# Selected tokens in quadrants: scores and mix of the first gated feed-forward layer as 64-wide tiles of the array

## The reference

```python
B, T, _ = X.shape                       # 4, 512, 128; E = 8 experts, k = T // 8 = 64
logits = jax.nn.sigmoid(jnp.einsum('bth,eh->bte', X, Wr))
topk_vals, topk_I = jax.lax.top_k(logits.transpose(0, 2, 1), k)
Xg = jnp.take_along_axis(X, idx_flat[:, :, None], axis=1).reshape(B, E, k, H)
QKV = jnp.einsum('beki,eij->bekj', Xg, Wqkv)
# rope on the first 64 features of Q and K, by the position of the token
M = topk_I[..., :, None] >= topk_I[..., None, :]
scores = jnp.where(M, jnp.einsum('bekd,bemd->bekm', Q, K) / math.sqrt(HP), -jnp.inf)
AV = jnp.einsum('bekm,bemd->bekd', jax.nn.softmax(scores, axis=-1), V) * topk_vals[..., None]
Xpre = jnp.einsum('bekj,eji->beki', AV, Wo)
out = jnp.zeros((B, T, H)).at[jnp.arange(B)[:, None], idx_flat].add(Xpre.reshape(B, E * k, H))
```

## Time and profile before

| | us |
|---|---|
| median of 3 runs (lowest, highest) | 339.64 (338.06, 342.19) |
| the profiled execution | 338.87 |
| its span, first to last instruction | 337.1 |
| PE busy | 255.7 (76% of the span), 2153 matmul records |
| DVE, ACT, POOL busy | 220.8, 196.4, 168.0 |
| chain that ended last, by engine | PE 32%, POOL 22%, DVE 17%, issue 15% |

### The profile page before, as it was taken

How to read it: one execution, slowest core, us unless ns; L and a number is a source line. 1 busy time by engine, 2 the same in 40 slices (tenths; PEclk the granted TensorE clock), 3 DMA queues, 4 the chain that set the end, 5 groups by cost and what they waited for, 6 DMA issues and landing times.

```text
span 337.1 us, 7069 instructions
## 1 busy us (share of the span) xinstructions
PE 255.7 (76%) x2153; PEld 202.8 (60%) x2153; DVE 220.8 (66%) x691; ACT 196.4 (58%) x454; POOL 168.0 (50%) x207
## 2 busy tenths in 40 slices
PE   2699985399899886999989842612999999998600
PEld 1488865155677654677758631211799999997400
DVE  2356409897677764788899866820387676677555
ACT  1564579969677668876855542400576667665220
POOL 2512339980222528524014687760048788888611
PEclk9999999599999999999989655755899999999955
DMA  7780000640000000000000011342123222211083
GB/s 202 236 346 3 2 1 1 213 147 0 3 1 2 2 1 0 3 0 2 0 3 26 33 42 55 106 128 64 50 73 81 65 77 77 77 36 39 0 280 93
DMA packets 21458, 21.64 MB, mean 64 GB/s; under 512 B 3360, under 2 KB 19106, under 8 KB 20784
## 3 DMA queue, kind: packets, MB, share of 16 engines
q1 hardware_dynamic: 18784, 16.79, 16.3%
q0 software_dynamic: 2496, 4.26, 4.0%
q10 hardware_dynamic: 144, 0.15, 0.2%
HBM read 14.68 MB, written 7.42 MB: 66 GB/s over the span
## 4 chain that ended last, share of the span: by engine, by line
PE 32%; POOL 22%; DVE 17%; issue 15%; ACT 6%; DMA 6%; SPq 1%; POOLq 0%; DVEq 0%
PE bank L1148 25%; POOL expert_rows L815 12%; POOL dispatched_rows L791 8%; DVE x L1139 2%; DMA region_q<-expert_rows 2%; DVE region_k L884 2%; DVE top L883 2%; DVE region_p L897 2%; POOL rstd L733 2%; DMA x<-in 1%; DVE nm L970 1%; DVE region_k L972 1%; DMA dispatched_rows<-region_t,slot 1%; PE bank L1201 1%; PE bank L1184 1%
## 5 line engine op out<-in xcount | busy, mean ns | idle before, releaser
L1148 PE MATMUL bank<-w_scaled,w_high 128*128 128x256 f16 x276 | 48.2, 279 | 1.0 <-ACT w_scaled L687 1.0
L815 POOL DMA_INDIRECT expert_rows<-region_k,slot_dest x24 | 29.5, 1230 | 28.3 <-DVE region_k L1121 21.3
L791 POOL DMA_INDIRECT dispatched_rows<-region_t,slot x32 | 32.1, 1002 | 16.7 <-issue 9.2
L1148 PE MATMUL bank<-w_scaled,w_low 128*128 128x256 f16 x138 | 38.5, 279 | 0.0
L1148 PE MATMUL bank<-w_high,region_k 128*128 (+1 forms) x308 | 31.7, 222 | 8.1 <-DVE region_k L1088 6.6
L687 ACT ACTIVATE w_scaled<-bank 128x512 f16<-128x512 f16 x23 | 13.7, 597 | 37.9 <-PE bank L1455 37.8
L1124 DVE TENSOR_TENSOR region_k<-region_x,region_k 128x768 f16<-128x768 f32 x23 | 22.0, 958 | 19.2 <-ACT region_k L692 19.2
L1148 PEld LDWEIGHTS bank<-w_high,region_k 128*128 128x128 f16 x308 | 25.3, 99 | 10.7 <-DVE region_k L1088 8.3
L815 POOL DMA_INDIRECT expert_rows<-region_x,slot_dest x22 | 27.4, 1246 | 6.7 <-issue 6.7
L742 POOL TENSOR_TENSOR w_low<-w_scaled,w_high 128x512 f16<-128x512 f32 (+1 forms) x23 | 27.3, 1209 | 5.5 <-ACT w_high L529 5.3
L731 POOL TENSOR_SCALAR minus_mean_rstd<-mean_var 128x4 f32<-128x4 f32 x16 | 3.1, 192 | 52.7 <-DVE mean_var L843 36.4
(11 more groups left out here) (238 smaller groups left out, 735.1 us busy)
## 6 DMA issues: line engine op xcount, KB each, us to landing
w_scaled<-in SPq DMA_DIRECT2D x5, 1024.0 KB, 8.1
w_scaled<-dispatched_rows SPq DMA_DIRECT2D x23, 131.0 KB, 2.3
region_q<-expert_rows SPq DMA_DIRECT2D x4, 512.0 KB, 5.6
dispatched_rows<-pad_rows SPq DMA_DIRECT2D x18, 65.5 KB, 2.9
x<-in SPq DMA_DIRECT2D x4, 256.0 KB, 4.6
region_w<-in SPq DMA_DIRECT2D x2, 512.0 KB, 6.9
out<-x SPq DMA_DIRECT2D x4, 256.0 KB, 2.5
w_scaled<-in SPq DMA_DIRECT2D x1, 704.0 KB, 4.1
```

The lines of the kernel that those rows point to most:

```text
L791: pool.indirect_dma_start(disp, bass.IndirectOffsetOnAxis(slot[:, b * T + t, c:c + 1].bitcast(U32), 0), pay[:, b * T + t, :], None).then_i ...
L815: pool.indirect_dma_start(ytok, bass.IndirectOffsetOnAxis(dst[:, n, h:h + 1].bitcast(U32), 0), yv[n % 4][:, h * D:(h + 1) * D], None, boun ...
L1148: return pe.matmul(o, l, r, start=start, stop=stop)
```

## The change

The two halves of a pair are kept apart in the array. The scores are two matmuls of 64x64 (128 rows, 64 columns of the array each), the mix two matmuls of 64 rows and 64 columns: the first batch's in the upper left quadrant's rows, the second batch's in the lower rows, each into the half of the partitions that the other does not write. So the second batch (b odd) of an expert lands in the other half of the partitions of `yh` and `yl` than before, and `pickt` must have the two experts of a pair swapped for b odd: there the four turning matmuls of a tile become eight with 64 columns of weights each. One wait on PE's own semaphore is added ahead of each fourth mix (q == 2). DVE, ACT, POOL and SP keep their instructions, in the same order.

```diff
@@ stage of the one-hots
                     for p in range(E // 2):
-                        last = mm(bank[6 + t % 2][:, p * P:(p + 1) * P], pick[:, n, p * P:(p + 1) * P], ident16)
+                        o = bank[6 + t % 2][:, p * P:(p + 1) * P]
+                        if b % 2 == 0:
+                            last = mm(o, pick[:, n, p * P:(p + 1) * P], ident16)
+                        else:
+                            for i in range(2):
+                                c = p * P + (1 - i) * J
+                                last = mm(o[i * J:(i + 1) * J, :], pick[:, n, c:c + J], ident16)
@@ scores
                     mm(o, identbf, causal, True, False)
-                    mm(o, qkt[:, q, 0:P], qkt[:, q, P:2 * P], False, True).then_inc(slot_scores, 1)
+                    for i in range(2):
+                        r = slice(i * J, (i + 1) * J)
+                        last = mm(o[r, r], qkt[:, q, r], qkt[:, q, P + i * J:P + (i + 1) * J], False, True)
+                    last.then_inc(slot_scores, 1)
@@ mix
                     if q == 0:
                         wait(pe, mixed_low, g - 1)
+                    elif q == 2:
+
+                        pe.wait_ge(slot_mixed, n)
                     for i in range(2):
                         b = 2 * h + i
-                        last = mm(bank[6 + g % 2][J * (e % 2):J * (e % 2 + 1), b * D:(b + 1) * D],
-                                  etl[:, q, i * J:(i + 1) * J], vv[:, q, :])
+                        r, c = slice(i * J, (i + 1) * J), (e + i) % 2 * J
+                        last = mm(bank[6 + g % 2][c:c + J, b * D:(b + 1) * D], etl[r, q, r], vv[r, q, :])
                     last.then_inc(slot_mixed, 1)
```

## The result

| | before | after |
|---|---|---|
| median, 9 runs each on one chip (lowest, highest) | 339.6 (338.06, 342.19) | 341.7 (340.49, 344.3) |
| the profiled execution, its span | 338.87, 337.1 | 343.78, 342.0 |
| matmul records of PE, PE busy | 2153, 255.7 | 2217, 259.2 |

The ratio of the times is 1.0072, with a 95% interval of 1.0041 to 1.0103: after takes 1.4 to 3.5 us more, some 2.4, which is within 2%. The forecast was 343.0, with a range of 339.5 to 346.0.

What follows compares the result with a forecast made beforehand. PE's time was taken to bound one-hots and pairs. Turning +3.7 us, scores and mix -0.2 over eleven periods, last pairs -0.1: +3.4, taking the median from 339.64 to 343.0 us, range 339.5 to 346.0.

Steps and rivals of the forecast that it cites:

- the prediction's own signs: Profile after: tiles at 1.35 us and period 2.02 expected; tiles at 1.1 or periods at or below 1.9 would refute.
- part 1: Narrow turning of the one-hots for batches 1 and 3: +0.48 us a tile over 8 tiles, +3.7 in all.
- part 2: Scores in halves, from mask step to their end: 0.34 us before, 0.43 after, +0.09 a pair.
- Part 3: Mix in halves: second batch's first record overlaps first batch's second, -0.11 us a pair; bounds 0 and -0.22.
- A change of shape costs 0.15 us: On PE, between matmuls of different tile shape: 0.15 us with an f32 load behind, 0.11 back to f16.
- rivals B: Column halves overlap as well: turning +2.0 us, pairs gain 0.075 each, +1.1 in all, 340.7; chance 0.13.
- rival C: Halves are independent arrays in loads and matmuls: -0.24 us a pair, -0.9 in all, 338.7; chance 0.08.
- Part 4: Wait for slot_mixed ahead of four mixes: asks for the previous pair's mix, long met, costed at nothing.
- No change of the clock: One-hots and pairs stay as dense as before, so the granted clock stays at 1.00 (2.4 GHz) there.
- rival E: Half-filled array lowers the granted clock in the pairs: period up by about 1.2 us, +14, 357; chance 0.03.

Runs made afterwards that it cites:

- e3: Before with only the scores in two halves of the width, mix and turning as before: 338.42 us, ratio 0.9979.
- e5: After with the mix over all 128 rows, each half in its own columns, the same shape as the scores: 341.67 us, ratio 1.0074.
- e1: After with the full-width turning of before, so only scores and mix in halves: 338.21 us, ratio 0.9991.
- e6: e5 without narrow turning: router columns swapped for odd batches, ACT and DVE copying gathered tokens back into place: 338.31 us, ratio 1.0004.
- e2: Before with only the new half-width turning, scores and mix as before: 340.58 us, ratio 1.0044.
- e7: e6 plus eight matmuls that do nothing useful, in PE's waits in the last two pairs: 336.46 us, ratio 0.9929.
- e4: After plus eight idle-time matmuls ahead of scores and mixes in the last two pairs: 339.41 us, ratio 1.0015.
- e9: Before plus the same eight idle-time matmuls in the last two pairs, nothing else: 339.47 us, ratio 1.0037.

## Why the prediction came out as it did

The total came out right by luck, since errors under it cancelled: two terms were too high, and one was missing. Two of the prediction's own signs said so: tiles at 1.10 us, where 1.1 was to make part 1 wrong, and a period of 1.82, where 1.9 or less was to make part 2 or 3 wrong.

**A change of shape costs 0.15 us: right with an f32 load behind it.** In after it stands at five places: mask step to scores, scores to mix, mix to et, gathers to narrow turning and back. The load came 0.16, 0.15, 0.20, 0.31 and 0.15 us behind the start of the last record, whose stream takes 0.055, 0.055, 0.11, 0.22 and 0.055, so 0.09 to 0.11 us pass each time with nothing streaming; the rest of the 0.15 is the bare load. In the one-hots, where loads are f16, the two changes of a tile were counted at 0.26, and the whole tile grew by 0.23. The Trainium skill (TensorEngine Tiling (Array Packing), Key Properties) says that a change of tiling mode drains the engine, and the traces agree. Where shapes were made alike the cost went (e3, e5: 0.11 from the scores' first load to the mix's, 0.27 in after). That e3 gains by it was not seen beforehand: I had counted a new change ahead of the scores, and not that the one behind them would go. In after it does not go, because the mix there uses 64 rows and the scores 128.

**Part 1, +0.48 a tile, +3.7 in all: mis-sized.** Measured: +0.23 a tile, +1.8. The step that failed is "four matmuls more at 0.055: 0.22". The column halves run at the same time, and eight matmuls of 64 columns take what four of 128 take. I had that as the lower bound, +2.0, of rivals B and C.

**Part 2, +0.09 a pair: wrong in size**, for the same reason: the two halves' four records take 0.11, not 0.22, and from the mask step to the mix's load it is 0.43 where it was 0.44. **Part 3, -0.11 a pair: wrong in size.** It rested on "PE starts matmuls in order". They start in order and still do not wait: 0.05 us behind the first load two loads and two records of the mix have started, and the mix is shorter by 0.22 (0.65 to 0.43). Together -0.22 a pair, against the -0.02 of the forecast. That is rival C, whose chance I put at 0.08. By the Trainium skill (TensorEngine Tiling (Array Packing), Key Properties) tiles load and multiply in parallel; the traces agree. The rule of its Gotcha 1 that spoke against it, on two row tiles and one PSUM bank, is not what the trace shows: in after the two halves of the mix write one bank and overlap, in 0.43 us for the four records.

**Part 4, the wait for slot_mixed at nothing: right.** The only wait that a mix shows in the trace of after is for ACT's copy, behind the last pairs' scores.

**No change of the clock: wrong**, and this is what made the total right. I looked at rows 2 for whether the stages stay dense, and they do, at 1.00. I did not ask what lies behind the stage. A shorter PE sequence with the same chain over ACT and DVE leaves PE more pauses in the last pairs, and in the traces of after, e1, e3, e5 and e6 the clock fell at the end of the pairs; in those of before and e2 it did not. That the pauses bring the fall is shown as far as filling them goes: e7 against e6 in the medians, e4 against after in the traces. It is 2.2 us behind the last mix in after, 2.4 by comparison with e4. My rival E had the clock, and put it inside the pairs, at +14.

**The sum with measured terms**: +1.8 for the turning, -2.3 for the pairs, +2.2 for the clock gives +1.7 us, and the measurement says 1.4 to 3.5. The 0.6 of the clock's late return in the one-hots is not in it, since e7 and e9 show it without the new turning. e1 (-0.3, interval -1.3 to +0.7) and e2 (+1.5, 0.7 to 2.3) add up to +1.2, which agrees with the measured 2.4 only within their intervals. Rival C with -0.9 in all had the mechanism of the halves; it lacked the clock, and with 2.2 for it would have read 340.9.

The floor of 1.82 was in no rival either. I had read 5.8 and 4.8 us of slack for DVE and ACT off their busy time in rows 2; that says nothing of how long the loop over them is, which left 0.22 us a pair. After sits on it, so a price on PE behind the scores is no longer a price in time. It is why the 0.14 that e5 saves from the scores to et brings nothing.

## What to carry to other kernels

Two matmuls in different column or row-and-column halves of the array run at the same time, loads too, so what counts is the number of changes of shape (some 0.11 to 0.15 us each, on the way in and on the way out). The scores in halves bring 0.01 us a pair where the mix behind them has another shape (after), and 0.16 where it has the same one (e3). When a stage bound by PE is made shorter, look next at how long the loop over the other engines is, since the gain ends there (1.82 us here). Then look at the work behind the stage: with more pauses in its last, draining iterations the granted clock fell over that work, which took back 2.2 of the 2.3 us that the pairs had gained. And where an edit needs its data in another order, make the order where it is small (the router's 8 columns) and not where it is multiplied (8 tiles of turning): the trace of e6 shows 0.1 us for it where after pays 1.8.

## What the runs showed of the hardware that I had not expected

- Column halves and quadrants of the array take their loads and their streams together: eight loads of 64 f16 columns in 0.25 us, four of 64 f32 columns in 0.20, where two of 64 f32 columns in one half took 0.19. The f32 matmuls' two records go in pairs too.
- Two halves writing into one bank at the same time do not hold each other up (the mix of after and of e5, 0.43 and 0.39 us for four records).
- The granted clock fell from 2.4 to 1.2 GHz behind a stage in whose last four pairs PE waited six times for 0.16 to 0.53 us, and the same 32 matmuls took 3.62 us in place of 1.96. The Trainium skill (TensorE: Matmul & The Clock Gate, Part 1) says that the clock is set by how busy PE has been of late; e4 against after, and e7 against e6, agree. What exactly brings it down these traces do not settle.
